# Decoder layer on one core: weights first, gate split on GpSimd, VectorE's list at the seam reordered, late transfers on GpSimd's queue

## What is computed

```python
x = x + L0_attn(layernorm(x))            # Wq Wk Wv Wo G1 G2 gamma beta theta
x = x + L0_xattn(layernorm(x), ctx)      # w_q w_kv w_proj w_rel
x = x + L0_ffn(layernorm(x))             # w_gate w_up w_down
# L0_attn: no softmax
q, k, v = silu(x @ Wq), silu(x @ Wk), x @ Wv
q, k = lrpe(q, theta), lrpe(k, theta)    # [t*cos(theta*pos), t*sin(theta*pos)]
energy = einsum('bhnd,bhmd->bhnm', q, k) * tril
out = (energy @ v) @ Wo * sigmoid(x @ G1 @ G2)
out = layernorm(out) * gamma + beta
# L0_xattn
logits = q k^T / sqrt(32) + (i - j) * w_rel[head];  out = (softmax(logits) @ v) @ w_proj
# L0_ffn: activations rounded to 127 levels a row, weights to -1, 0, 1 times their mean
out = bitlinear(silu(bitlinear(x, w_gate)) * bitlinear(x, w_up), w_down)
```

## Time and profile before

| | |
|---|---|
| median of 3 runs | 1256.83 us (1255.55 to 1259.95) |
| the profiled execution | 1259.24 us, its span 1257.4 us |
| PE busy | 1174.2 us, 93% of the span |
| PE weight loads | 903.6 us, 72% (beside the matmuls) |
| DVE, ACT, POOL busy | 809.4 (64%), 588.0 (47%), 541.6 us (43%) |
| granted TensorE clock, mean | 0.982 |

### The profile page before, as it was taken

The page is one execution under the profiler, slowest core; times in us unless marked ns, Lnnn a source line. Parts: engine busy times, 40 slices in busy tenths (PEclk is TensorE's granted clock), DMA queues, the critical chain, the costliest instruction groups (busy, mean ns, idle before and its releaser), DMA issues. The chain is left out here.

```text
span 1257.4 us, 25102 instructions
## 1 busy us (share of the span) xinstructions
PE 1174.2 (93%) x9456; PEld 903.6 (72%) x9482; DVE 809.4 (64%) x1492; ACT 588.0 (47%) x967; POOL 541.6 (43%) x432
## 2 busy tenths in 40 slices
PE   3799999999799999999999999999999988899997
PEld 3687888887677878778877878878788866344443
DVE  5856666676546666656566665656665677587774
ACT  3222332225235445435444454444454566577775
POOL 0012111115116665656665665765755212354551
PEclk9899999999989999999999999999999989899999
DMA  5311333425524253343343343352532683122121
GB/s 173 96 49 47 102 127 127 143 79 165 134 74 114 51 149 96 73 125 89 80 133 98 82 133 86 97 138 52 134 101 60 202 247 113 42 73 67 58 67 42
DMA packets 76138, 129.43 MB, mean 103 GB/s; under 512 B 18764, under 2 KB 35276, under 8 KB 76027
## 3 DMA queue, kind: packets, MB, share of 16 engines
q1 hardware_dynamic: 63267, 104.28, 30.0%
q0 software_dynamic: 11680, 21.81, 5.4%
q10 hardware_dynamic: 1104, 2.15, 0.6%
HBM read 68.96 MB, written 11.22 MB: 64 GB/s over the span
## 5 line engine op out<-in xcount | busy, mean ns | idle before, releaser
L1761 DVE TENSOR_REDUCE xa_m_part<-xa_psM 112x1 f32<-112x376 f32 x512 | 266.5, 545 | 232.8 <-PE xa_psM L1968 230.3
L1652 ACT ACTIVATE space<-xa_psS 125x448 f32<-125x448 f32 x384 | 208.2, 544 | 180.7 <-PE xa_psS L1952 178.9
L1543 POOL TENSOR_TENSOR xa_sum_space<-xa_sum_space,space 125x896 f32<-125x896 f32 x112 | 238.3, 2128 | 97.3 <-ACT space L1652 92.9
L1968 PE MATMUL xa_psM<-xa_k,xa_q 104*112 104x376 f32 x512 | 162.2, 355 | 16.1 <-DVE xa_m_part L1761 7.6
L1952 PE MATMUL xa_psS<-xa_q,xa_k 104*125 104x224 f32 x768 | 147.3, 274 | 3.4 <-ACT space L1652 3.4
L1952 PEld LDWEIGHTS xa_psS<-xa_q,xa_k 104*125 104x125 f32 x768 | 139.1, 189 | 6.7 <-ACT space L1652 4.5
L1968 PEld LDWEIGHTS xa_psM<-xa_k,xa_q 104*112 104x112 f32 x512 | 87.9, 177 | 36.8 <-DVE xa_m_part L1761 12.9
L1526 POOL TENSOR_SCALAR xa_oT_hi<-xa_o_f 128x224 fp32r<-128x224 f32 x32 | 25.3, 790 | 180.7 <-DVE xa_o_f L1777 180.5
L1992 PE MATMUL xa_psO<-space,cv 125*32 125x224 f32 x1536 | 95.2, 360 | 0.9 <-ACT space L1652 0.9
L1938 PE MATMUL xa_psR<-xa_cT_hi,w_lo 128*128 128x376 f32 x256 | 91.6, 358 | 0.0
L1938 PE MATMUL xa_psR<-xa_cT_hi,w_hi 128*128 128x376 f32 x256 | 86.9, 339 | 1.7 <-DVE xa_cT_lo L1751 1.7
(11 more groups left out here) (214 smaller groups left out, 2662.0 us busy)
## 6 DMA issues: line engine op xcount, KB each, us to landing
xa_k<-xa_k_st SPq DMA_DIRECT2D x378, 94.0 KB, 2.2
xa_q<-xa_q_st SPq DMA_DIRECT2D x192, 56.0 KB, 2.0
cv<-in_ctx_dram POOLq DMA_DIRECT2D x7, 1500.0 KB, 21.5
cv<-in_L_ffn_w_gate_dram SPq DMA_DIRECT2D x14, 512.0 KB, 4.7
cv<-in_L_ffn_w_down_dram SPq DMA_DIRECT2D x10, 512.0 KB, 7.0
cv<-in_L_ffn_w_up_dram SPq DMA_DIRECT2D x9, 512.0 KB, 6.0
sa_x_raw<-in_x_dram SPq DMA_DIRECT2D x8, 448.0 KB, 6.1
sa_rows<-in_x_dram SPq DMA_DIRECT2D x8, 448.0 KB, 4.0
```

The costliest lines, as they stand in the source:

```text
L1543: nc.gpsimd.tensor_tensor(p_sum[:], before, tile, ALU.add).then_inc(p_summed, 1)
L1652: nc.scalar.activation(pT[:, (s + i) % 2, j], psS[0:KB, (HG * i + j) % EXP_BANKS, 0:2 * N], ACT.Exp).then_inc(exp_done, 1)
L1761: V.tensor_reduce(m_part[:, t, jj, seg:seg + 1], psM[0:T, seg, 0:SEG], AX.X, ALU.max).then_inc(mx_read, 1)
L1968: M.matmul(psM[0:T, seg, 0:SEG], q4[0:ROWS, g, jj, t * T:(t + 1) * T], k4[0:ROWS, g % 2, jj, seg * SEG:(seg + 1) * SEG], start=True, stop= ...
```

## The change

It has four parts.

1. Start of self-attention. SP's queue loads x, Wq, Wk, theta, G1, G2, then Wv and Wo (each behind its split as before), then gamma and beta with a semaphore of their own, then x of batch 1. The split of G1 and G2 goes to POOL, but for the last two subtractions. `make_tables` is cut in two, `make_angles` before `split_weight(2)` and `reduce_angles` behind it; `split_weight(3)` moves behind `rotate(2)`.
2. Rows and bias. Cut in two and put behind `rotate(1)` and `rotate(2)` of DVE's iteration 1.
3. Seam. DVE's `statistics(0)` goes behind the take of r5, `sa_finish(B - 1)` from Xa to q0, `statistics(1)` to K1a, `normalise(1)` to q2, `split_weight(3)` behind half 3 of the first maxima.
4. Last batch and feed-forward. The three loads of units 8 to 10 and the six packings go from ACT's to POOL's queue, each set with one semaphore. xq is made on DVE, behind the third product of a tile, and the end of the attention's list on DVE is reordered.

```diff
...
+            def load_weight(n):
...
+                if n >= 2:
+                    sp.wait_ge(w_split_lo, n - 1)
+                sp.dma_start(w_raw[:, n % 2], (Wq, Wk, Wv, Wo)[n].rearrange("(k p) n -> p k n", p=P)).then_inc(w_in[n % 2], DMA)
...
             load_x(0)
+            load_weight(0)
+            load_weight(1)
...
                          allow_slow_non_contiguous=True).then_inc(theta_in, DMA)
-            for n, w in enumerate((Wq, Wk, Wv, Wo)):
-                if n >= 2:
-                    sp.wait_ge(w_split_lo, n - 1)
-                sp.dma_start(w_raw[:, n % 2], w.rearrange("(k p) n -> p k n", p=P)).then_inc(w_in[n % 2], DMA)
-                if n == 0:
-                    sp.dma_start(g1_raw[:], G1.rearrange("(k p) n -> p k n", p=P)).then_inc(small_in, DMA)
-                    for r in range(HG):
-                        sp.dma_start(g2_raw[HD * r:HD * (r + 1), :], G2).then_inc(small_in, DMA)
-                    sp.dma_start(gamma_b[:], gamma.partition_broadcast(T)).then_inc(small_in, DMA)
-                    sp.dma_start(beta_b[:], beta.partition_broadcast(T)).then_inc(small_in, DMA)
+            sp.dma_start(g1_raw[:], G1.rearrange("(k p) n -> p k n", p=P)).then_inc(small_in, DMA)
+            for r in range(HG):
+                sp.dma_start(g2_raw[HD * r:HD * (r + 1), :], G2).then_inc(small_in, DMA)
+            load_weight(2)
+            load_weight(3)
+            sp.dma_start(gamma_b[:], gamma.partition_broadcast(T)).then_inc(affine_in, DMA)
+            sp.dma_start(beta_b[:], beta.partition_broadcast(T)).then_inc(affine_in, DMA)
+            load_x(1)
...
             for b in range(B):
-                if b + 1 < B:
+                if 1 <= b < B - 1:
...
+            def split_gate_weights():
+                pool.wait_ge(small_in, (1 + HG) * DMA)
+                for k in range(KT):
+                    wide = g1_raw[:, k].unsqueeze(1).broadcast_to([P, HG, HD])
+                    nc.gpsimd.tensor_scalar(g1[:, 0, k].rearrange("p (r e) -> p r e", r=HG), wide, 1.0, None, ALU.mult)
+                nc.gpsimd.tensor_scalar(g2[:], g2_raw[:], 1.0, None, ALU.mult).then_inc(g_split, 1)
+                pool.wait_ge(g_split, 1)
+                for k in range(KT):
+                    wide = g1_raw[:, k].unsqueeze(1).broadcast_to([P, HG, HD])
+                    last = nc.gpsimd.tensor_tensor(g1[:, 1, k].rearrange("p (r e) -> p r e", r=HG), wide,
+                                                   g1[:, 0, k].rearrange("p (r e) -> p r e", r=HG).bitcast(F32), ALU.subtract)
+                last.then_inc(g_split, 1)
...
             rstd(0, x_mv, x_ve, x_rs, x_meanvar, x_veps, x_rstd)
-            pool.wait_ge(small_in, 7 * DMA)
+            split_gate_weights()
+            pool.wait_ge(affine_in, 2 * DMA)
...
+            def reduce_angles():
...
-            def split_gate_weights():
-                dve.wait_ge(small_in, 7 * DMA)
...
-                V.tensor_copy(g2[:], g2_raw[:]).then_inc(g_split, 1)
+            def split_gate_rows():
                 dve.wait_ge(g_split, 1)
...
-            def iteration(b, u, gated=None, last=False):
+            def iteration(b, u, gated=None, last=False, between={}):
...
                         rotate(g, b + 1, u)
+                        if g in between:
+                            between[g]()
                     split_t(b + 1)
...
+            def make_rows():
+                dve.wait_ge(rows_made, 2)
+                dve.wait_ge(wr_in, DMA)
+                V.tensor_copy(key_row, key_i)
+                V.tensor_scalar(one_row, key_i, 0.0, 1.0, ALU.mult, ALU.add)
+                V.tensor_scalar(zero_row, key_i, 0.0, None, ALU.mult)
+                V.tensor_copy(xpos, xpos_i).then_inc(bias_step, 1)
+                V.tensor_scalar(wr[:, 1:2], wr[:, 0:1], -1.0, None, ALU.mult).then_inc(bias_step, 1)
...
+            def make_bias():
+                dve.wait_ge(bias_step, 2)
+                for c, (src, col) in enumerate(((ones[HD:HD + H, 0:1].broadcast_to([H, N]), 1), (xpos, 0))):
+                    V.tensor_scalar(bias[:, 2 * c], src, wr[:, col:col + 1], None, ALU.mult).then_inc(bias_step, 1)
+                for c, (src, col) in enumerate(((ones[HD:HD + H, 0:1].broadcast_to([H, N]), 1), (xpos, 0))):
+                    dve.wait_ge(bias_step, 4)
+                    V.scalar_tensor_tensor(out=bias[:, 2 * c + 1], in0=src, scalar=wr[:, col:col + 1], in1=bias[:, 2 * c].bitcast(F32),
+                                           op0=ALU.mult, op1=ALU.subtract).then_inc(bias_step, 1)
...
             turn_x(1, 0)
+            make_angles()
             split_weight(2)
-            make_tables()
-            split_gate_weights()
+            reduce_angles()
+            split_gate_rows()
...
             rotate(0, 0, u)
-            split_weight(3)
...
             rotate(2, 0, u)
+            split_weight(3)
...
             iteration(0, uses(1))
-            iteration(1, uses(2, 1), uses(1))
...
+            iteration(1, uses(2, 1), uses(1), between={1: make_rows, 2: make_bias})
...
         def round_x(i):
+            if not is_first(i):
+                pool.wait_ge(xq_ready, i)
...
             nc.gpsimd.tensor_scalar(xm[:], xn[:], x_scale[:], MAGIC, ALU.mult, ALU.add).then_inc(xm_ready, 1)
-            if not is_first(i):
-                pool.wait_ge(xq_turned, i)
-            wait_apart(pool, xm_ready, i + 1, pool_passed)
-            nc.gpsimd.tensor_scalar(xq[:], xm[:], MAGIC, QMAX, ALU.subtract, ALU.min).then_inc(xq_ready, 1)
-            pool.wait_ge(xq_ready, i + 1)
+            pool.wait_ge(xm_ready, i + 1)
...
+        def round_x(i):
+            dve.wait_ge(xm_ready, i + 1)
+            wait_count(dve, xq_turned, i)
+            V.tensor_scalar(xq[:], xm[:], MAGIC, QMAX, ALU.subtract, ALU.min).then_inc(xq_ready, 1)
...
             hidden(i + 1, 2)
+            if prep:
+                round_x(i + 2)
...
+        def round_second_x():
+            round_x(1)
...
         def rest():
-            hidden(0, 2)
...
     SPLIT_HI_AT = {"K0a": 2, "q3": 3}
-    SPLIT_LO_AT = {"q0": 2, "q3": 3}
+    SPLIT_LO_AT = {"q0": 2}
...
+            def load_freed():
...
+                for unit in FREED:
+                    dst, src = ffn_part(unit)
+                    pool.wait_ge(full[bank_of["K3b", B - 1]], use_of["K3b", B - 1])
+                    pool.dma_start(dst, src).then_inc(f_freed, DMA)
...
+            def pack_last_keys():
...
+                for j in (2, 3):
+                    for what in ("K3a", "K3b"):
+                        pool.wait_ge(read[bank_of[what, B - 1]], use_of[what, B - 1])
+                    pool.wait_ge(st_full, UNITS * (NG * (B - 1) + 1) + LAST_STEP + j + 1)
+                    for r, part in enumerate((0, 1, 0)):
+                        pool.dma_start(k4[HD * r:HD * (r + 1), 1, j, :].bitcast(F32),
+                                       k_st[HD * j:HD * (j + 1), part, :].bitcast(F32)).then_inc(last_packed, DMA)
...
                     act.wait_ge(w_scale_step, 3)
-                act.wait_ge(f_in[r], DMA * (raw_use[unit] + 1))
+                if unit in FREED:
+                    act.wait_ge(f_freed, len(FREED) * DMA)
+                else:
+                    act.wait_ge(f_in[r], DMA * (raw_use[unit] + 1))
...
                             take_shift(NG * b + s + 1)
-                        if b == B - 1 and s == 1 and k in FREED_AT:
-                            for unit in FREED_AT[k]:
-                                dst, src = ffn_part(unit)
-                                act.wait_ge(full[bank_of["K3b", B - 1]], use_of["K3b", B - 1])
-                                act.dma_start(dst, src).then_inc(f_in[raw_of[unit]], DMA)
-                        if (b, s, k) == (B - 1, 1, 13):
-                            for j in (2, 3):
...
                     sa_gate_output(0)
-                if what == "r5":
+                if what == "K0a":
                     statistics(0)
-                if what == "K0a":
...
                     sa_centre(B - 1)
-                if what == "Xa":
+                if what == "q0":
                     sa_finish(B - 1)
+                if what == "K1a":
+                    statistics(1)
+                if what == "q2":
+                    normalise(1)
...
                 take(what, 0)
-            statistics(1)
-            normalise(1)
...
                 reduce_half(0, half)
+                if half == 3:
+                    split_weight(3)
...
             ffn_statistics(1)
-            for c in range(2):
-                ffn_hidden(0, c)
+            ffn_hidden(0, 0)
+            ffn_second_x()
+            ffn_hidden(0, 1)
+            ffn_round_second_x()
+            ffn_hidden(0, 2)
...
                 take(what, B - 1)
-            ffn_second_x()
...
                 if t == 0 and seg == 0:
-                    pe.wait_ge(k_packed[g % 2][jj], KPACK * (n // 2 + 1))
+                    if n == NG * B - 1 and jj >= 2:
```

(3 more changed lines are left out.)

55 lines of the change are left out of this document (17 added, 38 removed).

## The result

The changed kernel takes 1245.99 us in the median of 13 runs (12 of them 1242.73 to 1251.86; one stood far off at 2859.4, and without it the median is 1245.5), the kernel before 1256.44 in 13 runs beside it. The ratio is 0.9917, 95% interval 0.9901 to 0.9933: 10.4 us faster, where 24.4 were forecast, and 13.6 us above the forecast of 1232.4. The profiled execution took 1244.26 us, span 1242.6, against 1259.24 and 1257.4. The time lies above the stated range of 1221 to 1243.

The account below looks back on a forecast made before the run. The prediction took TensorE, busy 1174.2 of 1257.4 us, as the bound, so only its idle or slow-clock time could be won. Terms 6.2 + 1.9 + 5.0 + 2.0 + 4.4 + 4.9 = 24.4 gave a 1232.4 us median, range 1221 to 1243.

Follow-up runs that it names:

- the wait on the seam: The changed kernel, with GpSimd issuing load_context(1) only when the twelve packed-query transfers of the first pair have landed: 1230.49 us, ratio 0.9797.

## What to carry to other kernels

When work is moved ahead on one engine, list each DMA that stands behind it in its queue, and ask what is in flight at the time to which it moves. The price of such a meeting is read from issue to landing of the small transfer that somebody waits for, never from how long its issue takes. A prefetch that nobody needs yet (here the load issued at 319.57 is first read by PE at 386.72) is made to wait for the urgent transfers, and issued in two or three parts.

## What the runs showed of the hardware

A load of 1500 KB on GpSimd's queue raised the landing of 56 KB packings on SP's queue from at most 3.5 to 13.3 us, while SP's issues stayed as fast (7.95 and 7.74 us for twelve). The Trainium skill ("DMA: Bandwidth & Descriptors", Queues, rings and completion order) says that each DMA engine takes turns between queues packet by packet, and that a completion's increment lands only behind every earlier write of that engine, whatever its queue. The second rule would fit landings that are late by so much. The first rule doesn't say by itself that one transfer and six pieces of it must cost the same, 11.8 and 7.2 us in the runs, since their packets differ: on GpSimd's queue the same 1.54 MB went as 1216 packets in one transfer and as 480 in six (318 to 353 us). But two pieces have 1248 packets and yet free the main loop of its waits, so the packets aren't the whole of it either. Neither rule was isolated here.

In two pieces the same load no longer makes PE wait for keys in the main loop (3.6 us in five waits with one transfer and the wait on the seam, 0.2 us in one with two). It is also in sooner, 14 to 16 us instead of 21 to 24. Six pieces of one block each lengthen GpSimd's DRAIN at the end of the program from 2.36 to 6.69 us, in both kernels that had them.

Of nine issues on GpSimd's queue the two that met VectorE's 128x1024 float-to-bfloat16 pass from SBUF took 0.93 and 0.69 us instead of 0.72 and 0.50, and ended 0.14 and 0.10 us behind the pass; issues beside its passes of that size from PSUM took the usual 0.50. The Trainium skill ("SBUF — State Buffer", SBUF: two separate sides) has GpSimd locked out while VectorE runs in a fast mode, and its queue's transfers waiting for descriptors. These two issues agree with it, if the pass is in such a mode, which no run here shows. The cost was that of the passes met, 0.4 us in all.
